# A four-layer graph network: eight scatter semaphores, a constant count column, and both last-layer subtractions on GpSimd

## What is computed

```
x = layernorm(x + segment_sum(x[src], dst))                              # layer 0
m = relu(x[src] + edge_attr);  h = (1+eps)*x + segment_sum(m, dst)       # layer 1
x = layernorm(x + relu(relu(h @ W1.T + b1) @ W2.T + b2))
z = segment_sum(x[dst] * edge_weight, src)                               # layer 2
x = layernorm(x + z @ weight)
deg = segment_sum(1, src);  d = where(deg > 0, deg**-0.5, 0)             # layer 3
gate = sigmoid(x[src] @ w_src + x[dst] @ w_tgt + bias)
x = layernorm(x + segment_sum((d[src]*d[dst]*gate)[:, None] * x[src], dst))
```

## Time and profile before

| | us |
|---|---|
| median of 3 executions | 8055.8 (8040.68 to 8060.42) |
| the profiled execution: its own time | 8085.47 |
| its span, first to last instruction | 8083.7 |
| TensorE busy | 5818.8 (72% of the span) |
| VectorE busy | 6912.9 (86%) |
| ScalarE busy | 3967.8 (49%) |
| GpSimd busy | 4145.9 (51%) |
| mean granted TensorE clock | 0.835 of full speed |

### The profile page before, as it was taken

One profiled execution on the slowest core, in us unless ns is written; L12 is line 12 of the kernel. 1 busy time (PEld: TensorE's weight loads), 2 busy tenths in 40 slices (PEclk: granted clock), 3 DMA queues, 4 the chain that ended last, 5 costly groups with the idle time before them and its releaser, 6 DMA issues. The chain is left out here.

```text
span 8083.7 us, 287895 instructions
## 1 busy us (share of the span) xinstructions
PE 5818.8 (72%) x120824; PEld 5437.1 (67%) x120824; DVE 6912.9 (86%) x8082; ACT 3967.8 (49%) x5752; POOL 4145.9 (51%) x3710
## 2 busy tenths in 40 slices
PE   5767775888885666666653255777777749999995
PEld 4666664777775666666653255777777749999995
DVE  8999998999996999998974347889889888999994
ACT  2333332444442555555542226889999853333331
POOL 4555777777777777777777730000000005666662
PEclk8888887999997888888776666777778769999996
DMA  7866212777773777777764324666666626666661
GB/s 127 148 119 119 42 27 59 174 175 175 175 175 95 210 207 205 208 209 205 210 173 120 91 78 158 204 207 212 213 209 216 203 99 215 201 204 201 202 202 43
DMA packets 1123439, 1316.76 MB, mean 163 GB/s; under 512 B 581317, under 2 KB 869253, under 8 KB 1122183
## 3 DMA queue, kind: packets, MB, share of 16 engines
q1 hardware_dynamic: 768861, 739.56, 33.3%
q10 hardware_dynamic: 250536, 508.89, 22.0%
q0 software_dynamic: 103168, 54.68, 2.8%
HBM read 902.26 MB, written 400.43 MB: 161 GB/s over the span
## 5 line engine op out<-in xcount | busy, mean ns | idle before, releaser
L675 POOL DMA_INDIRECT slot_table<-recs,idx_now x3224 | 3280.9, 1018 | 1349.9 <-issue 879.0
L1547 PE MATMUL banks<-hot_d,msg 128*96 128x256 bf16 x10192 | 1547.4, 307 | 1044.5 <-DVE msg L1032 836.2
L1547 PEld LDWEIGHTS banks<-hot_d,msg 128*96 128x96 bf16 x10192 | 1262.2, 136 | 1185.3 <-DVE msg L1032 874.0
L686 POOL TENSOR_TENSOR msg_z<-left,msg_z 128x448 bf16<-128x448 f32 x364 | 816.7, 2244 | 2387.6 <-ACT msg_z L1389 2387.6
L950 DVE TENSOR_TENSOR hot_d<-lodl,banks 128x2560 bf16<-128x2560 bf16 (+1 forms) x884 | 1487.6, 1683 | 0.0
L1356 ACT CAST far_now<-hot_td 128x3584 fp8e4<-128x3584 bf16 x364 | 1154.7, 3172 | 34.7 <-DVE hot_td L969 33.3
L1320 ACT CAST near_now<-hot_t 128x1792 fp8e4<-128x1792 bf16 x364 | 613.9, 1686 | 1035.5 <-DMA source_marks<-near_now 596.2
L1601 PE MATMUL banks<-x_win,hot_td 128*128 128x32 bf16 x30576 | 883.4, 182 | 222.9 <-issue 208.5
L1601 PEld LDWEIGHTS banks<-x_win,hot_td 128*128 128x128 bf16 x30576 | 831.6, 100 | 249.0 <-issue 234.4
L1289 ACT CAST msg<-banks 128x480 bf16<-128x480 f32 (+1 forms) x1040 | 522.1, 554 | 631.5 <-PE banks L1547 593.6
L961 DVE TENSOR_TENSOR hot_t<-lo_bc,banks 128x1280 bf16<-128x1280 bf16 (+1 forms) x884 | 807.9, 914 | 10.1 <-DMA lo_bc<-row_table 10.0
(11 more groups left out here) (190 smaller groups left out, 9974.9 us busy)
## 6 DMA issues: line engine op xcount, KB each, us to landing
lo_bc<-row_table ACTq DMA_DIRECT2D x364, 448.0 KB
dl_bc<-row_table SPq DMA_DIRECT2D x364, 448.0 KB, 4.6
target_marks<-far_now SPq DMA_DIRECT2D x364, 448.0 KB, 3.1
dl_bc<-target_marks SPq DMA_DIRECT2D x364, 448.0 KB, 4.2
lo_bc<-row_table ACTq DMA_DIRECT2D x468, 320.0 KB
slot_table<-zeros SPq DMA_DIRECT2D x52, 1617.0 KB, 10.8
rec_in<-slot_table ACTq DMA_DIRECT2D x364, 231.0 KB
source_marks<-near_now ACTq DMA_DIRECT2D x364, 224.0 KB
```

The source lines that it names most:

```text
L675: pool.indirect_dma_start(out=slot_dram[c.number], out_offset=bass.IndirectOffsetOnAxis(ap=idx_now[:, c.slot, g:g + 1], axis=0), in_=recs[ ...
L686: pool.tensor_tensor(msg3[:, blk.slot, :, 2 * D:3 * D], left3[:, blk.slot], msg3[:, blk.slot, :, D:2 * D], ALU.subtract).then_inc(msg_made ...
L1547: mm = t.matmul(banks[0:3 * D, 6 + blk.par, 0:WIN], rows[:, blk.slot, g, :], hot[:, blk.slot, g // 2, :, g % 2], start=(blk.b == 0 and g = ...
```

## The change

Four edits:
1. `LANES` goes from 4 to 8: eight semaphores take turns, so up to eight scatter DMAs are under way.
2. The count column of `msg_z` is set to 1.0 once before the targets stage; the 14-column comparison in `make_hot_s` goes for each of 364 blocks. An empty slot has no match in the one-hot matrix, so its 1.0 is summed nowhere.
3. In the gated stage `make_hot_d` compares with the counting row in PSUM (`far_d`, bank 5), as the sources and the edges stages do, no longer with `iota_d` in SBUF.
4. In the gated stage GpSimd makes `left3` too. `msg3` becomes a view on `hot_td` with 128 columns for each group, of which the last 32 are zeroed once; the scatter matmuls of this stage load 128 columns of weights and write 128 rows.

```diff
-LANES = 4
+LANES = 8
...
-        msg3 = msg_z[:, :, :, 0:3 * D]
+        msg3 = hot_td[:, 0].rearrange("p k (g f) -> p k g f", f=P)
...
             def sum_gated():
+                def make_left(blk):
+                    pool.wait_ge(first_made[3], blk.number + 1)
+                    pool.tensor_tensor(left3[:, blk.slot], total3[:, blk.slot], msg3[:, blk.slot, :, 0:D], ALU.subtract
+                                       ).then_inc(rest_made[3], 1)
+
+                pool.sem_inc(rest_made[3], 2)
+                make_left(Block(0, 0))
                 for blk, more in straight():
+                    if more >= 1:
+                        if blk.number:
+                            pool.wait_ge(msg_made[3], blk.number)
+                        make_left(blk.ahead(1))
                     pool.wait_ge(second_made[3], blk.number + 1)
                     pool.tensor_tensor(msg3[:, blk.slot, :, 2 * D:3 * D], left3[:, blk.slot],
                                        msg3[:, blk.slot, :, D:2 * D], ALU.subtract).then_inc(msg_made[3], 1)
...
-                steps = iota_d[:, :, :] if q == 3 else far_d
+                steps = far_d
...
+                v.memset(msg_z[:, :, :, D], 1.0)
+                dve.drain()
                 first = Block(0, 0)
...
-                v.tensor_scalar(msg_z[:, blk.slot, :, D],
-                                lodl[:, bass.ds(blk.chunk, 1), HB + blk.h0:HB + blk.h0 + BG].rearrange(
-                                    "p c g -> p (c g)"), 0.5, None, ALU.is_ge).then_inc(hot_d_made[2], 1)
...
                 start_sweep(3)
+                v.tensor_copy(banks[:, 5, 0:WIN], words_of(iota_d))
+                v.memset(msg3[:, :, :, 3 * D:P], 0.0)
+                dve.drain()
...
                     dve.wait_ge(gated, blk.number + 1)
+                    dve.wait_ge(rest_made[3], blk.number + 1)
...
-                    dve.wait_ge(first_made[3], blk.number + 1)
-                    part = lambda q: msg3[:, blk.slot, :, q * D:(q + 1) * D]
-                    v.tensor_tensor(left3[:, blk.slot], total3[:, blk.slot], part(0), ALU.subtract
-                                    ).then_inc(rest_made[3], 1)
...
-                    act.wait_ge(rest_made[3], blk.number + 1)
+                    act.wait_ge(rest_made[3], blk.number + 3)
                     s.copy(msg3[:, blk.slot, :, D:2 * D], left3[:, blk.slot]).then_inc(second_made[3], 1)
...
-                    mm = t.matmul(banks[0:3 * D, 6 + blk.par, 0:WIN], rows[:, blk.slot, g, :],
+                    mm = t.matmul(banks[0:rows.shape[-1], 6 + blk.par, 0:WIN], rows[:, blk.slot, g, :],
```

More of the change, by code:

```diff
@@ L1109, in sum_gated @@
                         add_sums(3, agg3, blk.chunk, 1 - blk.par, blk.number + 1)
-                    dve.wait_ge(rest_made[3], blk.number + 1)
                 add_sums(3, agg3, NCH, 1, BLOCKS + 2)
@@ L1606, in scatter @@
                 def scatter(blk):
-                    pe.wait_ge(hot_d_made[2], 2 * blk.number + 2)
+                    pe.wait_ge(hot_d_made[2], blk.number + 1)
                     pe.wait_ge(msg_made[2], blk.number + 1)
```

## The result

The changed kernel takes 8359.6 us (median of 4 executions, 8336.0 to 8360.2) against 8055.8 us before: a ratio of 1.037, 95% interval 1.035 to 1.040. It is slower by 304 us. 8292 was forecast, within 8110 to 8410. The profiled execution took 8359.74 us, its span 8358.0, 274.3 more than the span before.

A forecast was written before the change was run, and what follows sets the result against it. It took TensorE to pace the gated stage, scatter DMAs the edges' end, and a ring of engines the targets. -318 - 15 + 570 = +237 on 8085.5 gives 8322, less 30 for the median: 8292 us, range 8110 to 8410.

The forecast's parts named there:

- Edit 1, -318 us: Edges stage: eight semaphores remove the waits for scatter landings, its second stretch falling from 605 to 287 us.
- the upper bound: Edges stage: the full gain from eight semaphores, 318 us, beyond which the stage's own loop decides.
- the lower bound: Edges stage: heavy early transfers keep their pace, their 257.3 us of waits before 1000 us stay, 128 us go.
- Rival B: Scatter DMAs land later in proportion, as if the queue had a fixed pace: 8482 or 8610 us; chance 0.09.
- Edit 2, -15 us: Targets stage: dropping the count column's comparison saves VectorE 0.08 us a block, about half reaching the end.
- Edit 3, the subtraction from 2.25 to 1.01 us: Gated stage: with no VectorE instruction reading two SBUF tensors, each GpSimd subtraction takes 1.01 us.
- the closed chain: Gated stage: scatter, part 0, `left3`, part 2, next scatter close once a block, 4.61 us against TensorE's 3.47.
- Rival C: Gated stage: GpSimd's two subtractions overlap, costing less than 2.02 us; 7703 us if wholly hidden; chance 0.06.
- D: Gains and losses come out even, subtraction pair near 1.83 us at full clock: 8056 us; chance 0.03.
- Padding: Gated stage: 128-column weights save 0.04 us a block, for the first load, which isn't hidden.
- The clock, a third of the time at half speed, +0.47: Gated stage: TensorE's pauses lower its granted clock, adding 0.47 us to a block, giving 5.04.
- The sum: Whole kernel: edges -318, targets -15 and gated stage +570 give +237 us.

The follow-up runs named there:

- e1: Kernel before with eight scatter semaphores in place of four and nothing else, first chip: 11368.4 us against 11373.0, ratio 0.9993.
- e2: Changed kernel with GpSimd's part 2 of a block put ahead of `left3` of the next, first chip: 11322.0 us against 11373.0 for the kernel before.
- e3: Kernel before with only the gated stage's comparison reading its counting row from PSUM, first chip: 11336.7 us against 11373.0, ratio 0.9967.
- e5: Kernel before with eight scatter semaphores in place of four and nothing else, second chip: 7826.9 us against 8177.2, ratio 0.957.
- e4: Kernel before with only the count column filled once, first chip: 11363.6 us against 11373.0, ratio 0.9995.
- e12: Kernel before with six scatter semaphores in place of four, first chip: 11286.0 us against 11367.3, ratio 0.993.
- e11: Kernel of e2 with the gated stage's comparison reading its counting row from SBUF again, first chip, one execution: 11569.5 us.
- e9: Changed kernel with eight extra 128-row matmuls a block on TensorE in the gated stage, first chip, one execution: 11796.0 us.
- e6: Changed kernel with GpSimd making each `left3` subtraction twice, second chip, one execution: 9035.1 us.
- e8: Changed kernel with eight extra matmuls a block in the gated stage, using one row of zeros, second chip, one execution: 8410.1 us.

## Why the prediction was right

Its steps, each beside what the trace and the runs showed:

- **Edit 1, -318 us.** The edges' last block came 324 us earlier in the profiled execution. The waits on a landing fell to 72.1 us; the last DMA started at 4415.8 us, 20 later than the 4396 of the sum and 9 later than the edges want it (4407). ScalarE makes one stop of 23.6 us there; its other stops of this kind are under 5 us, and e1, where the scatter was over long before, has such short ones too. The choice of the upper bound was right: the waits on a landing before 1000 us, which the lower bound kept, fell from 257.3 to 60.2 us. One premise was too simple. The prediction took 5.12 us a block as the stage's own loop; in the runs of the first chip, whose scatter was over before, the first 308 blocks take 4.78 each (e1, e2, e3), so the scatter beside it seems to cost the stage some 0.3 us a block as well, with eight semaphores too (5.07 in the changed kernel). As the chips differ, and the targets stage does not (4.49 to 4.58 us a block on all), that is likely but not shown. Rival B (a queue of fixed pace) is out, by the changed kernel's trace and by e5.
- **Edit 2, -15 us.** A block of the targets stage takes 4.492 us in place of 4.518, -9 us, and alone (e4) it can't be told from nothing; neither can the 9 us, as kernels without the edit lie between 4.51 and 4.58 in this stage (e1, e3, e5, e12). The term was small enough for that not to matter.
- **Edit 3, the subtraction from 2.25 to 1.01 us.** 1.03 in the changed kernel, 1.02 with this edit alone, and e11 shows the hold-off in both directions. The section cited from the Trainium skill, SBUF — State Buffer, agrees with these numbers; that the second one waits for the first one's whole length is said there of instructions in two-port modes, and for this comparison with two SBUF inputs it is e11 that shows it. For the size, which it leaves open, the row of the one free subtraction was the right one.
- **Edit 4, the closed chain.** Of its links, by e9's rows, 1.89 was 1.86, 0.58 was 0.56, 0.07 was 0.14 (GpSimd started later behind ScalarE than in the row that was read), 2.02 was 2.03, 0.05 was 0.06: 4.65 us against 4.57. e2 shows that it was this chain and nothing else (3.35 us with the two instructions exchanged), e6 that what is put into it comes out at its end. Rival C, a pair that overlaps, is out, and D with it: 7204.37 to 7206.40 is 2.03.
- **Padding.** The 14 matmuls take 1.76 us at full clock for 1.79, so it brought 0.03 a block, 0.04 having been assumed. The 0.4 us that loads setting the pace would have given does not appear. Its 0.027 us a load was also read from an fp8 load against a bf16 one: the bf16 load of 128 columns takes 0.110 us in the changed kernel, where that of 96 took 0.122. The wider load is faster, as the section cited from the Trainium skill, TensorE: Matmul & The Clock Gate, has it, but by 0.012 us.
- **The clock, a third of the time at half speed, +0.47.** 0.83 was granted in the stage, half-speed stretches held 621 us of 1864, a third, and e9 puts the price at 0.48. The size was right, but it came by likeness to other stages, which had been granted between 0.77 and 1.00, so that it fits this well is in part luck. The reason given, TensorE's idle time, is not shown: in e8 that time was filled and the clock stayed at 0.84.
- **The sum.** The gated stage cost (5.126 - 3.460) x 364 = +606 us where +570 was forecast: 0.08 a block of that is the chain's links (30 us), of which the link from ScalarE to GpSimd is nearly all. In the spans -324 - 9 + 606 = +273, measured +274.

The forecast of 8292 is 68 us below the median. Half of that is the gated stage (+36). The rest is that the profiled execution before lay 30 us above its median, which was taken off, while the one after lies on its own.

## What to carry to other kernels

Before a unit of work is moved to an engine with idle time, write down what stands ahead of it and behind it there, and close the ring: here an engine with a third of its time free made the stage 600 us longer because the instruction that another engine waited for stood behind one that waited for the block after. Let what releases the bound engine go first. And where such a ring leaves TensorE waiting, ask for the granted clock too: at the lower one the links on TensorE are longer, which was 174 us of 606 here.

## What the hardware showed that was not expected

**A sort stage of three and a half times the length on one chip.** In every kernel on the first chip, that of before included by its time, TensorE's matmuls of the sort come late, and the waits view names no engine or DMA for it ("issue"). The waits of TensorE in e3 (whole span), largest first, and the windows of the sort in e3 and in the changed kernel:

```profile
PE banks L1459 <- issue: 1671.5, 936, 4.6
PE banks L1452 <- issue: 793.3, 74, 84.2
```

```profile
100.00:5000.00 4900.00, 1203.23 (x12479) 870.84 (x12475) 1155.37 (x849) 447.76 (x948) 3102.88 (x3245) 0.57 0.22 39
```

```profile
100.00:1300.00 1200.00, 860.48 (x12193) 771.03 (x12190) 1130.61 (x832) 407.53 (x929) 895.79 (x873) 0.85 0.57 95
```

The same 12,000 matmuls take 4900 us in place of 1200, with TensorE, VectorE and ScalarE mostly idle. It was seen with four, six and eight semaphores, so it isn't the number of scatter DMAs under way. In e3's sort stage VectorE and ScalarE also waited 1348.2 and 1462.5 us for something that the view calls "remote", so TensorE's issue need not be where it starts. The cause stays open.

**Two kinds of extra matmuls, two clocks.** With eight matmuls of one row of zeros a block (e8) TensorE was busy 98% of the stage and was granted 0.84, as without them; with the same number of 128-row matmuls (e9) it was busy 95% and was granted 1.00. The two differ in rows, in values, in the columns of the weights (96 and 128) and in the chip, with one execution each; which of them matters wasn't taken apart.
